# Moving the router's choice, spline and last norms of a batch into the last steps of the next batch's attention 2, and the context projections between the heads of attention 1

## What is computed

```python
x = _layernorm(x + attn(x))                   # attention 1
x = _layernorm(x + xattn(x, ctx))             # attention 2: causal + cross
# the router part, on xf = x:
cluster_gates = _calibrate(xf @ cluster_sigs.T, knots, temperature)
cluster_idx = argmax(cluster_gates)
sel_gates = tile_gates[cluster_idx]           # 8 of the 64 calibrated tile scores
tile_idx = cluster_idx * 8 + argmax(sel_gates)
h = gelu(xf @ w1 + b1);  comp = tanh(h @ w2 + b2)
hh = relu(comp @ spline_w1[tile_idx] + spline_b1[tile_idx])
mag = hh @ spline_w2[tile_idx] + spline_b2[tile_idx]
y = xf + mag * directions[tile_idx] * output_scale
y = layernorm(y) * gamma + beta
x = _layernorm(x + y_minus_x)                 # written out as a second norm of y
```

## Time and profile before

| What | Value |
|---|---|
| Median of three runs | 2743.55 us |
| Lowest and highest | 2738.71 and 2749.35 us |
| The profiled execution, its own time | 2742.63 us |
| Its span, first to last instruction | 2740.7 us |
| TensorE busy | 2496.3 us (91%) |
| VectorE busy | 1901.8 us (69%) |
| ScalarE busy | 1377.0 us (50%) |
| Mean granted clock of TensorE | 0.92 |

### The profile page before, as it was taken

One profiled execution on the slowest core, in us unless ns is written; L12 is line 12 of the kernel. 1 busy time (PEld: TensorE's weight loads), 2 busy tenths in 40 slices (PEclk: granted clock), 3 DMA queues, 4 the chain that ended last, 5 costly groups with the idle time before them and its releaser, 6 DMA issues.

```text
span 2740.7 us, 43870 instructions
## 1 busy us (share of the span) xinstructions
PE 2496.3 (91%) x13339; PEld 1174.5 (43%) x13378; DVE 1901.8 (69%) x5254; ACT 1377.0 (50%) x2945; POOL 197.8 (7%) x353
## 2 busy tenths in 40 slices
PE   5899989999899988999889998899989999889994
PEld 2354334553345433454334543345433454334432
DVE  6668568684776848678386883958848586585844
ACT  2635655355553556335563464724656246563561
POOL 2010000100001000110001100011000110000000
PEclk8899988998889998899889998899988999989996
DMA  4500033000330004200042000510015000240000
GB/s 130 100 9 1 9 62 77 9 1 9 70 69 9 1 10 85 62 1 1 10 93 54 1 2 13 105 39 2 1 31 97 20 2 1 42 89 8 1 1 8
DMA packets 284183, 91.63 MB, mean 33 GB/s; under 512 B 269344, under 2 KB 279712, under 8 KB 283936
## 3 DMA queue, kind: packets, MB, share of 16 engines
q1 hardware_dynamic: 283936, 88.60, 15.8%
HBM read 17.27 MB, written 4.19 MB: 8 GB/s over the span
## 4 chain that ended last, share of the span: by engine, by line
PE 76%; DVE 11%; ACT 7%; issue 5%; DMA 1%; DVEq 0%; POOL 0%; SPq 0%; ACTq 0%; POOLq 0%
PE bank L1265 18%; PE bank L1049 15%; PE bank L1313 12%; PE bank L1299 9%; PE bank L1261 4%; PE bank L1296 3%; ACT work L522 3%; PE bank L1150 3%; DVE work L660 3%; PE bank L1140 2%; PE bank L1206 2%; PE bank L1157 2%; PE bank L1321 1%; ACT work L563 1%; PE bank L1278 1%
## 5 line engine op out<-in xcount | busy, mean ns | idle before, releaser
L563 ACT ACTIVATE work<-bank 128x512 f32<-128x512 f32 (+3 forms) x1536 | 743.4, 554 | 594.0 <-PE bank L1296 274.5
L914 DVE TENSOR_REDUCE top_half<-bank 128x1 f32<-128x512 f32 x1024 | 625.2, 679 | 18.5 <-PE bank L1265 18.5
L1265 PE MATMUL bank<-k_c,q_c 32*128 32x512 f32 x2048 | 625.9, 631 | 0.0
L1299 PE MATMUL bank<-q_c,k_c 32*128 32x512 f32 x2048 | 580.9, 645 | 19.9 <-ACT work L563 19.9
L522 ACT ACTIVATE work<-work,neg 128x512 bf16<-128x512 bf16 x512 | 362.5, 709 | 78.7 <-DVE work L660 44.0
L1265 PEld LDWEIGHTS bank<-k_c,q_c 32*128 32x128 f32 x2048 | 272.4, 183 | 222.5 <-DVE top_half L914 142.2
L660 DVE TENSOR_SCALAR_CACHE_REDUCE work<-bank 128x512 bf16<-128x512 f32 x512 | 321.7, 685 | 50.4 <-PE bank L1140 50.3
L1313 PE MATMUL bank<-work,v_flat 128*32 128x512 f32 (+3 forms) x3072 | 328.5, 570 | 6.1 <-ACT work L563 6.0
L911 DVE CUSTOM_DVE_ANT_0 masked<-bank,mask_w 128x384 bf16<-128x384 f32 (+3 forms) x512 | 224.6, 488 | 112.9 <-PE bank L1261 106.7
L1299 PEld LDWEIGHTS bank<-q_c,k_c 32*128 32x128 f32 x2048 | 253.8, 185 | 109.7 <-ACT work L563 74.2
L1296 PE MATMUL bank<-q_s,k_s 32*128 32x512 f32 (+3 forms) x1024 | 266.7, 480 | 0.0
(11 more groups left out here) (178 smaller groups left out, 2485.9 us busy)
## 6 DMA issues: line engine op xcount, KB each, us to landing
xT_pad<-xT SPq DMA_DIRECT2D x16, 256.0 KB, 2.8
ctx_sb<-ctxT SPq DMA_DIRECT2D x8, 512.0 KB, 3.6
x_res<-x SPq DMA_DIRECT2D x8, 512.0 KB, 5.1
out<-y_sb SPq DMA_DIRECT2D x8, 512.0 KB, 2.9
work<-work SPq DMA_TRANSPOSE x128, 4.3
qk_sb<-qkT SPq DMA_DIRECT2D x1, 512.0 KB, 4.8
wq_sb<-Wq SPq DMA_DIRECT2D x1, 512.0 KB, 7.0
wk_sb<-Wk SPq DMA_DIRECT2D x1, 512.0 KB, 7.2
```

What stands on the lines that cost most here:

```text
L563: nc.scalar.activation(pT[:, s % PT_SLOTS, g, q0:S], bank[:, RING + n % EXP_RING, 0:S - q0], ACT.Exp, scale=SCALE).then_inc(pT_ready, 1)
L914: nc.vector.tensor_reduce(top_half[:, i % 2, g, u // 2, u % 2:u % 2 + 1], scores, AX.X, ALU.max, negate=True).then_inc(slot_out, 1)
L1265: mm(dst, q_c[rows, i, P * t:P * (t + 1)], k_c[rows, i, S * half:S * (half + 1)], start=True, stop=True, tile_position=(GW * g, 0)).then_i ...
L1299: mm(dst, k_c[rows, i, P * u:P * (u + 1)], q_c[rows, i, :], start=True, stop=True, tile_position=(GW * g, 0)).then_inc(sT_mm, 1)
```

## The change

- The tiles' scores are copied out of PSUM at head 5 (`router_scores`), so that bank 7 is free. The gates and choice of the cluster stand at step 37 of attention 2 on VectorE, gates and choice of the tile at step 39, `expert_columns` at step 41, `gather` on TensorE at step 43, `compressed` and `spline` at 44, `third_sums` at 46; `third_norm` and `last_sums` stand before the last outputs, `last_norm` after them. The convolution and the bias addition stand at step 38 instead of 40.
- `expert_columns` and `gather` get their banks from the ring: one use and three uses more (`FFN_USES`). VectorE copies the expert columns, before it was ScalarE.
- The gelu stands at head 5 instead of 10 on ScalarE; `local_exps` at step 40 and `compress` at step 45.
- The context values stand on TensorE at heads 7, 9, 11 and 13, a key at each of the heads 8 to 15; VectorE and ScalarE empty bank 7 and bank 5 between the heads.
- The fillers stand at all heads from 2 on, eight up to head 6 and four from head 7 on. The exponentials of attention 1 have five slots instead of three.
- Scratch tiles of the router lie in `q_s` and `k_s`, idle in those steps; the output is stored from `k_s`, the last thing in SyncE's order of a batch, and ScalarE's next units wait for the store of the batch before.
- In the tail the same functions stand in the old order, with the copy of the scores added.

TensorE in attention 1 of batch 0, before: from the last head with fillers (k,q are the scores, work,v is `pv1`, ctx_sb the context).

The core of the diff:

```diff
-    A1_BANKS, E1_SLOTS = 4, 3
+    A1_BANKS, E1_SLOTS = 4, 5
     FILLERS = 8
+    EXPERT_STEP, GATHER_STEP = 41, 43
...
@@ slot_uses
+                if ffn and s == EXPERT_STEP:
+                    order.append(("expert",))
+                if ffn and s == GATHER_STEP:
+                    order.extend(("gather", i) for i in range(3))
...
@@ VectorE, new
+            def router_scores(c):
+                dve.wait_ge(gate_exp, c * 2 + 1)
+                nc.vector.tensor_copy(tile_scores, bank[:, 7, 0:NT * ST].rearrange("p (t n) -> p t n", t=NT)[:, :, CL:ST]).then_inc(tiles_in, 1)
+            def expert_columns(base, uses):
+                use = uses["expert",]
+                dve.wait_ge(slot_in, base + use + 1)
+                nc.vector.tensor_copy(expertT, slot(use)[0:TILES, :]).then_inc(slot_out, 1)
...
@@ ScalarE, batch
-                        if h == 6:
-                            local_exps(c)
-                        if h == 10:
-                            expert_columns(c)
+                        if h == 5:
                             hidden(c)
-                        if h == 13:
-                            compress(c)
+                    if 0 <= h - 7 < CTX_UNITS:
+                        context_key(h - 7)
...
                 for s in range(ALL_STEPS):
+                    if prev and s == 40:
+                        local_exps(c)
+                    if prev and s == GATHER_STEP + 2:
+                        compress(c)
                     probabilities(s)
...
@@ VectorE, batch, heads
-                        if h == 3:
-                            cluster_gates(c, sf)
-                        if h == 4:
-                            cluster_choice(c, sf)
-                        if h == 6:
-                            local_gates(c, sf)
-                        if h == 7:
-                            expert_choice(c, sf)
-                        if h == 11:
-                            compressed(c, sf)
-                        if h == 13:
-                            spline(c, sf)
+                        if h == 5:
+                            router_scores(c)
+                    if h in (6, 8, 10, 12):
+                        values((h - 6) // 2)
...
@@ VectorE, batch, steps
                 for s in range(ALL_STEPS):
-                    if s == ALL_STEPS - NC:
+                    if prev and s == 37:
+                        cluster_gates(c, sf)
+                        cluster_choice(c, sf)
+                    if s == 38:
                         if ahead == 2:
                             convolve(b + 2)
                         do(nc.vector.tensor_tensor(x_res[:], x_res[:], over_tiles(bp_row), ALU.add))
+                    if prev and s == 39:
+                        local_gates(c, sf)
+                        expert_choice(c, sf)
+                    if prev and s == GATHER_STEP + 1:
+                        compressed(c, base, uses)
+                        spline(c, sf, base, uses)
+                    if prev and s == GATHER_STEP + 3:
+                        third_sums(c, sf)
...
+                if prev:
+                    third_norm(c)
+                    last_sums(c, sf)
                 outputs(ALL_STEPS // BURST - 1)
                 finish(CROSS, HG - 1)
+                if prev:
+                    last_norm(c)
...
@@ TensorE, batch, heads
+                    if h in (7, 9, 11, 13):
+                        values((h - 7) // 2)
+                    if 0 <= h - 8 < CTX_UNITS:
+                        context_key(h - 8)
+                    keep_clock(7 if h < 4 else 6, FILLERS if h < 7 else FILLERS // 2)
...
@@ TensorE, batch, steps
+                    if prev and s == EXPERT_STEP:
+                        expert_columns(c, base, uses)
+                    if prev and s == GATHER_STEP:
+                        gather(c, base, uses)
```

269 lines of the change are left out of this document (134 added, 135 removed).

## The result

The changed kernel takes **2802.0 us** (median of 4 runs, 2798.9 to 2804.5) beside 2741.3 us for the kernel before (4 runs): ratio 1.0216, 95% interval 1.0191 to 1.0241. Forecast were 2711 us and a range of 2664 to 2760. It is outside, on the other side.

What follows compares the result with a forecast made beforehand. VectorE was taken to pace attention 1. Attention 1 -131, bridge clock +25, steps 37 to 40 +27, expert columns and gather +28, late clock +17.5, tail +1.5 summed to -32: 2711 us, range 2664 to 2760.

Steps and rivals of the forecast that it cites:

- What bounds the kernel: VectorE paces attention 1 (78.5 of 91 us busy); the change moves router work to last steps where VectorE idles.
- TensorE becomes the bound in heads 7 to 15.: Attention 1: TensorE sets the pace, 3.73 us for a head with a key, 4.66 with a pair as well.
- I add 1.5 for the wait of head 8's PV.: Attention 1, heads 8 to 14: 1.5 us added for head 8's PV waiting on ScalarE's copy.
- The transposing DMA 2.3.: End of attention 1: 2.3 us for the transposing DMA before the last PV, from ScalarE's wait of 2.19.
- Batch 0: Attention 1 of batch 0: the same steps reach 114.2 instead of 126.31, a gain of 12 us.
- The bridge's clock, +25: Last PVs, position and projection lose clock: 3 us for seven batches, 4 for batch 0; bounds -9 and +47.
- Steps 37 to 40, +27: Last group's rows wait behind router work and convolution on VectorE: 5.0 us in batches 1 to 5, 1.0 in 6 and 7.
- Expert columns and gather, +28: Steps 41 and 43: gather at full price 3.7 us on TensorE, transposes 0.3; 4.0 in each of seven batches.
- the clock, +17.5: Last steps: TensorE idle 6 us loses its clock, one PV burst and part of the scores slow, 2.5 us a batch.
- The tail, +1.5: Tail of the last batch: two more VectorE instructions on its chain, +1.5 us, bounds 0 and 2.5.
- (c): Rival, chance 0.15: TensorE becomes the bound in attention 1 and its half clock counts, 58 us over eight batches, 2769 us.
- (b): Rival, chance 0.15: clock lost at step 39 stays low to the end, 7.7 us in seven batches, 2747 us, no change.

Runs made afterwards that it cites:

- ctx_behind: Changed kernel with context values and keys back behind the heads of attention 1, eight fillers at heads 2 to 11: 2722.0 us, ratio 0.9950 to the kernel before.
- own_bank: Changed kernel with PV of heads 8 to 15 in PSUM bank 6 instead of 4, PV(8) moved behind head 13's fillers: 2755.4 us, ratio 1.0079.
- pos_early: Changed kernel with the next batch's position projection issued between PV(12) and PV(13) instead of behind PV(15): 2743.1 us, ratio 1.0021 to the kernel before.
- rows_first: Changed kernel with the cluster choice moved behind the last group's rows (step 39), convolution and bias to step 42: 2755.3 us, ratio 1.0067.
- conv_late: Changed kernel with only the convolution and bias moved to step 42, the whole choice staying at step 37: 2765.1 us, ratio 1.0089.
- no_gather: Changed kernel with choice behind the rows and convolution at step 42, plus 8 of the gather's 12 products left out: 2711.9 us, ratio 0.9877.
- ctx_rows_bank: Changed kernel with context behind the heads, choice behind the rows, convolution at step 42, and bank 6 for heads 8 to 15: 2687.0 us, ratio 0.9780.
- fill_gather: Changed kernel with late choice and convolution, own bank, early position and first query/key tile, plus four fillers ahead of each gather half: 2687.1 us, ratio 0.9810.

## Why the prediction was wrong, step by step

- **What bounds the kernel.** Right that VectorE paced the heads and that the router's work cost there: without it, with five exponential slots and nearly all else as before, the heads are 103 us shorter in all (ctx_behind). The slots alone are a part of it (batch 0 below).
- **"TensorE becomes the bound in heads 7 to 15."** The price of each head was right: predicted 3.73 and 4.66, measured 3.85 and 4.71. So the forecast was not missed here; it was missed by the two terms that follow. What the step left out bears on the change itself. I set the heads with the context against the old heads and asked whether each engine would fit. I did not ask what the heads would take with the router gone and the context left behind: 3.76, and that with eight fillers. Beside the wait of PV(8) and the bare end, the context's move was a loss of 85 us in the heads for 21 at the end.
- **"I add 1.5 for the wait of head 8's PV."** This is the first step that failed. The term was in the sum, with the right place, but mis-sized: 10.56 from head 13 to 14 instead of 4.66 + 1.5, so 4.4 too little in batch 4 (3.1 to 4.4 over the batches). What I left out is that a wait of TensorE here stops VectorE and ScalarE for 5.6 us, and that the clock halves behind it. own_bank prices the whole at 5.3 a batch where I had 1.5.
- **"The transposing DMA 2.3."** This is the second step that failed, in seven batches and in batch 0. I took it from ScalarE's wait of 2.19, which is only the rest of a transfer issued 2.2 us before that wait began. In the changed kernel the term measures 6.2 us: 1.8 in which the last transpose stood ready behind the one ahead of it, and 4.45 from issue to PV 15. PV 15 at half clock adds 0.7. From head 15's scores to position I had 10.8 us, and the trace 16.0. This 5.2, and the 5.0 between heads 8 and 15, is most of the 11.3 us by which batch 4 missed its 83.85 us to position (it took 95.2). pos_early, which puts work under these waits, wins 32.8 us in this stretch.
- **Batch 0.** I gave it 12 us. It got nothing (84.5 us from first scores to position before, 84.8 after): its heads had no router to lose and grew from 64.2 to 68.8 us, and its end has the same fault in the DMA. With the context behind the heads they are 58.0, so the five exponential slots alone are worth 6.2 there.
- **The bridge's clock, +25.** Wrong: 0.4 in the table, and position ran at full clock (3.70) behind the waits. The clock that fell with the last PVs (1.89 and 1.77) was back by then. A loss of clock was forecast at the right place with the wrong extent.
- **Steps 37 to 40, +27.** The wait was right (6.3 late forecast, 6.82 measured; about 2 in batches 6 and 7, measured 2.64). The discount for ScalarE's pace may not have been: rows_first won 7.0 a batch where I had charged 5.0, though PV 9's return to full clock is in that, and in batches 6 and 7 the wait was 2.64 where I had charged 1.0. In batch 0 attention 2 took 5.0 more, where I had charged nothing. Some 4 of these are not the change's: rows_first, conv_late and no_gather have the same instructions in batch 0, and took 192.4, 188.6 and 188.5 us for its attention 2, with 17.8, 7.0 and 7.0 us of half clock.
- **Expert columns and gather, +28, and the clock, +17.5.** Together 6.5 a batch, and no_gather prices two thirds of the gather with its clock at 6.3. The sum was near, but only half for my reason. I put the lost clock down to the 6 us wait, and behind it the clock did fall, to a PV 9 of 5.20 to 5.73. It fell a second time without a wait, ahead of the gather (1699.3), and that is the part that stays when the wait is gone (rows_first, 1672.3). The row that I had taken the rule from, 1436 to 1440, follows no wait of 6 us either: TensorE's longest there is 1.67. The gather at full price, 3.7, was too little, since it ran at half clock for all of its 7.1 us.
- **The tail, +1.5.** 1.5 (from PV 11 of batch 7 to the end 67.65 and 69.15 us).
- **Rivals.** (c) gave 2769 and was nearest in result; its mechanism, the same share of half clock in the heads, did not come: from 1430 to 1455 the trace has a clock of 1.00, and heads took over 4.7 us only at two waits (head 7 to 8, 5.34, behind 1.44 us for VectorE's copy of the router's scores, and head 13 to 14). (b), 7.7 a batch for the clock in the last steps, was nearly there (clock 0.72), but it was to end at no change since it kept the gain of attention 1.

The account: -32 forecast; attention 1 gained 86 less, the bridge lost 25 less, attention 2 lost 26 more, the start of the next batch 7 more. That is +62, and the spans differ by 62.0 (2802.7 and 2740.7).

## What to carry to other kernels

When a change has two parts, price each against the kernel with the other already made, not both against the old one; work that looks like a bare tail may be the cover of a transfer, and whoever takes it away must put something else there. Take a DMA's duration from issue to landing and ask what its queue does in between; a consumer's wait shows only the remainder. Where three engines take turns, a wait of one of them can cost its length, its clock and the stop of the other two: here 3.0 us cost 5.3. Where the engine that waits has the longest list behind it, the same repair can give nothing (ctx_rows_bank). And before a price of a few us is put on an edit, look at a batch that the edit does not touch.

## What the runs showed of the hardware that I had not expected

- Small products in different 32-row strips share the time of one (four instructions in 2.09 us), and a single full-size product between them takes that away (one instruction in 2.07 us, both at half clock). A filler is no neutral thing.
- The granted clock fell in stretches in which TensorE had no idle time at all (0.72 over 1669 to 1681 of rows_first, busy 12.00 of 12.00), and stayed at 1.00 in the same stretch with three quarters of the small gather products and half of the large ones left out. Fillers put behind the fall ran at half clock themselves, and the clock did not rise while they and the gather ran (0.50 over 1616 to 1628 of fill_gather).
- With the transposing DMAs the 16 DMA engines are busy for 0.53 of the time in attention 1 (batch 4 of the changed kernel). One takes 4.3 us from issue to landing, and with the next one ready its queue issued that 2.0 to 2.5 us later. A second queue for it was not tried: the Trainium skill ("DMA: Bandwidth & Descriptors", section "Silent corruption: two transposing streams in flight at once") says that two such streams in flight at once can corrupt each other, which no run here shows.
- The same instructions take different times by how often the clock falls under them: 26.15 or 27.84 us for the bridge, 188.5 or 192.4 us for attention 2 of batch 0.
- What stays open: why the clock falls more or less often in stretches where no instruction was moved (241.8 us of half clock against 186.5 when only the position projection is moved), and what the end of attention 1 would gain if ScalarE divided head 14's tile ahead of head 15's exponentials.
